# Full attention: values weighed for eight query blocks at once, in two part sums

## The reference

```python
qkv = h @ w_qkv.T                              # h: x after modulation
q, k, v = split(qkv, 3)                        # each (B, 16, T, 64)
s = q @ k.T * 64 ** -0.5 + rel_bias            # (B, 16, T, T); bias by clipped distance
p = softmax(s, axis=-1)
att = p @ v                                    # (B, 16, T, 64)
x = x + gate * (att.reshape(B, T, 1024) @ w_out.T)
```

## Time and profile before

| | |
|---|---|
| median of 3 runs | 2606.95 us (2600.77 to 2609.22) |
| the profiled execution | 2595.65 us, span 2593.9 us |
| busy over the span | PE 2449.6, PEld 1966.9, DVE 2153.8, ACT 2034.3, POOL 1519.8 us |
| stage of full attention | from 1655 to 2385.7 us of the span |
| mean granted TensorE clock | 0.986 |

### The profile page before, as it was taken

The page is one execution under the profiler, slowest core; times in us unless marked ns, Lnnn a source line. Parts: engine busy times, 40 slices in busy tenths (PEclk is TensorE's granted clock), DMA queues, the critical chain, the costliest instruction groups (busy, mean ns, idle before and its releaser), DMA issues. The chain is left out here.

```text
span 2593.9 us, 118567 instructions
## 1 busy us (share of the span) xinstructions
PE 2449.6 (94%) x52349; PEld 1966.9 (76%) x52349; DVE 2153.8 (83%) x2455; ACT 2034.3 (78%) x4077; POOL 1519.8 (59%) x1029
## 2 busy tenths in 40 slices
PE   6799999999999999999999999699999999997999
PEld 2478888888888888888888887467776776775787
DVE  5888888888888888888888886489898888885898
ACT  4788898889889899988888996667676666664776
POOL 3788887888888888888888884122222222222110
PEclk9999999999999999999999999899999999999999
DMA  3244433443444344334443332123232322221221
GB/s 96 51 99 94 109 78 93 94 108 84 98 94 111 82 94 99 95 84 94 101 97 83 91 85 60 43 48 68 46 70 50 67 47 66 51 57 31 83 74 41
DMA packets 275793, 202.01 MB, mean 78 GB/s; under 512 B 117568, under 2 KB 215880, under 8 KB 274248
## 3 DMA queue, kind: packets, MB, share of 16 engines
q1 hardware_dynamic: 275280, 194.42, 31.3%
HBM read 36.96 MB, written 1.11 MB: 15 GB/s over the span
## 5 line engine op out<-in xcount | busy, mean ns | idle before, releaser
L514 POOL TENSOR_TENSOR lt_t_sin<-lt_qk,lt_tab 128x512 f32<-128x512 f32 x384 | 685.1, 1805 | 225.1 <-DVE lt_qk L1296 222.8
L519 POOL TENSOR_TENSOR lt_qr<-lt_qr,lt_t_sin 128x1024 f32<-128x1024 f32 x192 | 457.7, 2384 | 28.1 <-POOL lt_t_sin L514 0.9
L2078 DVE TENSOR_REDUCE fa_neg_max<-bank 128x1 f32<-128x1024 f32 x256 | 301.6, 1220 | 90.7 <-PE bank L1875 89.1
L2000 ACT ACTIVATE fa_prob<-bank,fa_neg_max 128x1024 f32<-128x1024 f32 x128 | 142.6, 1114 | 215.7 <-DVE fa_neg_max L2078 163.4
L1901 PE MATMUL bank<-fa_prob_t,fa_v 32*64 32x128 f32 x16384 | 293.4, 276 | 16.8 <-issue 12.2
L1901 PEld LDWEIGHTS bank<-fa_prob_t,fa_v 32*64 32x64 f32 x16384 | 244.4, 130 | 78.1 <-issue 57.9
L2088 DVE STREAM_TRANSPOSE fa_prob_t<-fa_prob 128x1024 f32<-128x1024 f32 x256 | 302.1, 1218 | 0.0
L607 PE MATMUL bank<-lt_w_high,lt_x_high 128*128 128x512 f32 x576 | 262.2, 455 | 0.8 <-ACT lt_v_tok L1009 0.4
L977 ACT COPY lt_qk<-bank 128x512 f32<-128x512 f32 x384 | 224.5, 589 | 23.8 <-POOL lt_t_sin L514 2.8
L1296 DVE TENSOR_TENSOR lt_qk<-lt_qk,lt_rn 128x2048 f32<-128x2048 f32 x96 | 238.2, 2481 | 2.5 <-ACT lt_rn L1003 2.5
L1289 DVE TENSOR_REDUCE lt_ssq<-lt_qr 128x32 f32<-128x2048 f32 x96 | 218.9, 2281 | 24.7 <-ACT lt_qr L985 24.7
(11 more groups left out here) (260 smaller groups left out, 5857.0 us busy)
## 6 DMA issues: line engine op xcount, KB each, us to landing
lt_v<-lt_v_tok SPq DMA_DIRECT2D x576, 128.0 KB
fa_v<-fa_v_tok SPq DMA_DIRECT2D x256, 128.0 KB
lt_v<-lt_v_tok SPq DMA_DIRECT2D x192, 64.0 KB
lt_k_t<-lt_k_t SPq DMA_DIRECT2D x84, 128.0 KB, 2.9
lt_v<-lt_v SPq DMA_DIRECT2D x168, 64.0 KB, 2.1
lt_w_raw<-in_lt_wqkv_dram SPq DMA_DIRECT2D x36, 256.0 KB
ex_cw_all<-cw_kept SPq DMA_DIRECT2D x8, 1024.0 KB, 4.6
lt_x_s<-h_in SPq DMA_DIRECT2D x96, 64.0 KB, 2.8
```

The lines of the kernel that those rows point to most:

```text
L514: pool.tensor_tensor(dst[:, :, i, :], src[:, :, 1 - i, :], tab[:, g // 2 % 2, 1, at:at + 32].unsqueeze(1).to_broadcast([P, HEADS, 32]), AL ...
L519: pool.tensor_tensor(qr[:, g % 2, half], qr[:, g % 2, half], t_sin[:, :], ALU.add).then_inc(S.rotated, 1)
L2078: dve.tensor_reduce(neg_max[:, u % 2, par:par + 1], bank[:, 2 * par:2 * par + 2, :].rearrange("p a n -> p (a n)"), AX.X, ALU.max, negate=T ...
```

## The change

Values are weighed for a whole half (8 blocks) at once, a half late. A matmul has 256 moving columns in place of 128; a step has 32 of them in place of 64. The keys are summed in two parts of 512, each copied out by ScalarE (`empty_att`, at u % 4 of 3) into `h_mid`, a buffer that is free in this stage, and added by GpSimd before it divides. `prob_t` has one buffer in place of two, of the same size in all: step t of a half frees one eighth of it, and the next half's block t is written there, in a layout that alternates between even and odd halves. So `turn(u)` now waits at every step for the `weigh_v` of the same step. Projections come one at u % 4 of 0 (ahead of `weigh_v`), two at 2 and three at 3 (behind it); output products two at 1. Nothing cuts `weigh_v` any more. The reciprocals are turned once to a half and spread by transfers through memory (`widen_inverse`: 4 and 2 of them to a half), so `widen`, `spread_inverse` and `empty_inverse` are gone. There are 146 steps in place of 136.

```diff
-        prob_t = buf("prob_t", [P, 2, 2, UPQ, N])
...
+        prob_t = buf("prob_t", [P, 2, QB, QB, P])
...
         def jobs_at(u):
-            q, s = u // UPQ, u % UPQ
-            half = q // QPH + 1
-            if s == 1 or half >= HALVES:
+            half, first = u // QB + 1, (0, 1, 1, 3)[u % UPP]
+            if half >= HALVES:
                 return []
-            first = JPH * half + 6 * (q % QPH) + max(0, 2 * (s - 1))
-            return [first, first + 1]
+            first += JPH * half + 6 * (u % QB // UPP)
+            return [first + n for n in range((1, 0, 2, 3)[u % UPP])]
 
         def outs_at(u):
-            q = u // UPQ - 2
-            return [2 * q, 2 * q + 1] if u % UPQ == 1 and 0 <= q < QUADS else []
+            half = u // QB - (3 if u % QB == 1 else 2)
+            first = OUTS * half + (2 if u % QB == 1 else 0)
+            return [first, first + 1] if u % UPP == 1 and 0 <= half < HALVES else []
 
         def weighed_at(u):
 
-            q = u // UPQ - 1
-            return q if 0 <= q < QUADS else None
+            half = u // QB - 1
+            return half if 0 <= half < HALVES else None
...
-        STEPS = range(UNITS + 2 * UPQ)
...
+        STEPS = range(UNITS + 2 * QB + 2)
...
+                def widen_inverse(half):
+                    sp.wait_ge(S.inv_t, half + 1)
+                    if half >= 1:
+                        sp.wait_ge(S.inv_in, 32 * half)
+                    for a in range(4):
+                        sp.dma_start(inv_kept[:, 32 * a:32 * a + 32], inv_t[32 * a:32 * a + 2 * QB, :]).then_inc(S.inv_kept, 16)
+                    sp.wait_ge(S.inv_kept, 64 * (half + 1))
+                    if half >= 1:
+                        sp.wait_ge(S.att_t, half)
+                    for par in range(2):
+                        kept = inv_kept[QB * par:QB * par + QB, :].rearrange("(o u) q -> o (u q)", o=1)
+                        sp.dma_start(inv_all[HD * par:HD * par + HD, :], kept.to_broadcast([HD, N])).then_inc(S.inv_in, 16)
...
+                def divide(half):
+                    pool.wait_ge(S.att, 2 * half + 2)
+                    pool.tensor_tensor(att(1), att(0), att(1), ALU.add).then_inc(S.att_sum, 1)
+                    pool.wait_ge(S.att_sum, half + 1)
+                    pool.wait_ge(S.inv_in, 32 * (half + 1))
+                    if half >= 2:
+                        pool.wait_ge(S.out, OUTS * (half - 1))
+                    pool.tensor_tensor(att_t[:, half % 2, :].rearrange("p (u a r) -> p a u r", u=QB, a=4),
+                                       att(1).rearrange("p a (u r) -> p a u r", u=QB),
+                                       inv_all[:, :].rearrange("p (u a r) -> p a u r", u=QB, a=4),
                                        ALU.mult).then_inc(S.att_t, 1)
...
-                def weigh_v(q, s, n):
-
-                    half = q // QPH
-                    lo, step = KB // UPQ * s, KB // UPQ // 2
-                    if s == 0 and n == 0:
-                        pe.wait_ge(S.turned, 2 * UPQ * (q + 1))
-                        if q % QPH == 0:
-                            pe.wait_ge(S.v, 256 * (half + 1))
-                    for kb in range(lo + step * n, lo + step * (n + 1)):
+                def weigh_v(half, t):
+
+                    if t == 0:
+                        pe.wait_ge(S.turned, 2 * QB * (half + 1))
+                        pe.wait_ge(S.v, 256 * (half + 1))
+                    for i in range(KBS):
+                        kb, cols = KBS * t + i, slice(32 * i, 32 * i + 32)
                         for a in range(4):
                             rows = slice(32 * a, 32 * a + 32)
                             for par in range(2):
                                 d = slice(HD * par, HD * par + HD)
-                                mm = pe.matmul(bank[d, 4 + a, 0:P].rearrange("p (u r) -> p u r", u=UPQ),
-                                               v[rows, half % 2, kb, d],
-                                               prob_t[rows, q % 2, par, :, 32 * kb:32 * kb + 32],
-                                               start=kb == 0, stop=kb == KB - 1, skip_group_check=True)
-                    if n == 1:
-                        mm.then_inc(S.av, 1)
-
-                def spread_inverse(q):
-                    pe.wait_ge(S.wide_t, q + 1)
-                    if q == 0:
-                        pe.wait_ge(S.mean, 1)
-                    for a in range(4):
-                        rows = slice(32 * a, 32 * a + 32)
-                        for par in range(2):
-                            d = slice(HD * par, HD * par + HD)
-                            mm = pe.matmul(bank[d, 4 + a, P:2 * P].rearrange("p (u r) -> p u r", u=UPQ), mean_32[rows, :],
-                                           inv_t[rows, par, :, :], start=False, stop=True, skip_group_check=True)
-                    mm.then_inc(S.inv_all, 1)
+                                p = prob_t[rows, par, t, :, cols] if half % 2 else prob_t[rows, par, :, t, cols]
+                                mm = pe.matmul(bank[d, 4 + a, 0:JW].rearrange("p (u r) -> p u r", u=QB),
+                                               v[rows, half % 2, kb, d], p, start=kb % (KB // 2) == 0,
+                                               stop=kb % (KB // 2) == KB // 2 - 1, skip_group_check=True)
+                    mm.then_inc(S.av, 1)
...
-                    s, q = u % UPQ, weighed_at(u)
-
-
-                    fresh = s in (0, 3) or q is None
+                    s, half = u % UPP, weighed_at(u)
+
+
+                    fresh = s in (0, 3) or half is None
                     if u + 1 < UNITS:
                         scores(u + 1)
                     wait_emptied(pe, u - 1)
                     if s == 0:
                         for j in jobs_at(u):
                             job(j, fresh)
-
-                    outs, jobs = outs_at(u), jobs_at(u) if s >= 2 else []
-                    if q is not None:
-                        weigh_v(q, s, 0)
-                        if s in (1, 2):
-                            for n in outs[:1]:
-                                project_out(n, fresh)
-                            for j in jobs[:1]:
-                                job(j, fresh)
-                            outs, jobs = outs[1:], jobs[1:]
-                        weigh_v(q, s, 1)
-                        if s == 2:
-                            spread_inverse(q)
-                    for n in outs:
+                    if half is not None:
+                        weigh_v(half, u % QB)
+                    for n in outs_at(u):
                         project_out(n, fresh)
-                    for j in jobs:
-                        job(j, fresh)
+                    if s > 0:
+                        for j in jobs_at(u):
+                            job(j, fresh)
...
+                def empty_att(half, part):
+                    if half >= 1 and part == 0:
+                        act.wait_ge(S.att_t, half)
+                    act.copy(att(part), bank[:, 4:8, 0:JW]).then_inc(S.att, 1)
...
                 def turn(u):
-                    q = u // UPQ
-                    if u % UPQ == 0 and q >= 2:
-                        dve.wait_ge(S.av, UPQ * (q - 1))
+                    half, j = u // QB, u % QB
+                    if half >= 1:
+                        dve.wait_ge(S.av, QB * (half - 1) + j + 1)
                     for par in range(2):
                         dve.wait_ge(S.probs, 3 * u + 1 + 2 * par)
-                        dve.transpose(prob_t[:, q % 2, par, u % UPQ, :], prob[:, u % 2, par, :]).then_inc(S.turned, 1)
-
-                def invert(q):
-
-                    r = row_sum[:, q % 2, :, :]
-                    dve.wait_ge(S.probs, 3 * UPQ * (q + 1))
+                        if half % 2:
+                            dve.transpose(prob_t[:, par, :, j, :], prob[:, u % 2, par, :].rearrange("p (g n) -> p g n", g=QB))\
+                               .then_inc(S.turned, 1)
+                        else:
+                            dve.transpose(prob_t[:, par, j, :, :].rearrange("p g n -> p (g n)"), prob[:, u % 2, par, :])\
+                               .then_inc(S.turned, 1)
...
+                def turn_inverse(half):
+                    dve.wait_ge(S.inv, half + 1)
+                    if half == 0:
+                        dve.wait_ge(S.cleared, 1)
+                    else:
+                        dve.wait_ge(S.inv_kept, 64 * half)
+                    dve.transpose(inv_t[:, :], inv_sum[:, :]).then_inc(S.inv_t, 1)
...
+                    if u % QB == 0 and weighed_at(u) is not None:
+                        invert(weighed_at(u))
+                        turn_inverse(weighed_at(u))
```

146 lines of the change are left out of this document (56 added, 90 removed).

## The result

The kernel after the change takes **2626.5 us** (median of 5 runs, 2625.07 to 2629.82), the kernel before on the same chip 2600.77 (5 runs, 2599.34 to 2609.22). The ratio of the two is 1.0091, with a 95% interval of 1.0075 to 1.0108: the change made the kernel slower. The time lies in the range given; the ratio forecast was 1.0025.

A forecast was written before the change was run, and what follows sets the result against it. Bound: the chain of scores, maximum and exponential, a floor of 4.94 us a period (5.82 with bias). Steady +5, weighing +1, stalls -12, end +12.5 sum to +6.5 us: median about 2613.5, range 2599 to 2629.

The forecast's parts named there:

- the case with the largest chance: Whole kernel: slower than before by more than 0.3%, chance 0.43, against 0.41 within 0.3% and 0.16 faster.
- Weighing itself: `weigh_v` on TensorE: a wider piece costed at 2.02 us, 0 to 0.1 more, charged 1 us for the stage.
- The wait of a half's first step: VectorE waits 1.0 us for `weigh_v` before it may transpose, making that period 6.14 us.
- The fifth step's wait: The same wait at a half's fifth step costs nothing: bias moves the floor and there are no reciprocals.
- GpSimd's 5 us at the end of a half delay one low part: GpSimd's addition and product at a half's end: the delayed low part is wanted a step later, costed at nothing.
- The bias work: ScalarE rounds the bias behind three casts once to two halves, delaying an exponential about 0.5 us, 0.25 a half.
- Periods: Regular steps: floor of 4.94 us, 5.82 with bias, about 5.10 behind three projections; steady part +5 us.
- Stalls: Idle `weigh_v` matmuls released by nothing: half as many instructions leave more time per block, 12 of 13.3 us gone.
- The rival that they stay: Stalls in `weigh_v` are no matter of fetching or fall into longer matmuls too: +18.5 us, 2625, chance 0.22.
- The clock inside the loop: Sign of being wrong: a granted clock under full speed inside the loop.
- The end: Behind the last unit: eight pieces instead of four, 33 us against 20.3, +12.5 us.
- The start: Four more units without `weigh_v`, at the floor either way, clock already granted at 0.89: 0, give or take 1 us.

The follow-up runs named there:

- filling: Four matmuls of 256 columns, sums unread, added to each step without weighing: kernel after, 2623.38 us, ratio 1.0086; kernel before, 2594.06 us, ratio 0.9981.
- start and end mended: Kernel after with division, projection and small work moved, start filled, last output products in the scores' banks, last two divisions earlier: 2581.24 us, ratio 0.9914.

## Why the prediction was right, and where it was not

The median lies in the range, and the case with the largest chance, slower at 0.43, came. The mechanism of the regular periods and of the stalls was right, but that the time came out in the range was largely luck. The sum was +6.5 us, and it is +30.7 between the two profiled runs (+25.7 between the medians). The range reached so far up for stalls that stay; they went, and terms put at nothing or too low took their place. By its own steps:

- **Weighing itself**, 0 to 0.1 us a step more: it is 1.98 in place of 2.02, so the 1 us charged was not there. Halving the instructions alone doesn't shorten a piece.
- **The wait of a half's first step**: right in each number (copy 1.05, projection at 5.66, wait 1.0). The fifth step's wait costs nothing, as said.
- **"GpSimd's 5 us at the end of a half delay one low part"**, costed at nothing: this step failed, and it is the largest. Who waits for GpSimd was asked, and not whom its operations hold up. VectorE's addition does not end before GpSimd's product, 0.65 us in each of 14 halves, 9.1 in all; moving the product takes 9.3 back.
- **The bias work** was charged with 0.25 us a half, or 3.7; even halves take 1.27 more than odd ones, 8.9 in seven. ScalarE's rounding was counted about right: 0.60 in each of seven. VectorE's part was left out, 0.74 in each. About 0.5 of that is again GpSimd: a low part now falls beside the work and makes it 1.07 us in place of 0.58. The rest is lost cover: before the change the work fitted into a period of 5.35 that TensorE set, and now the period is 5.01.
- **Periods**: forecast 5.10 behind three projections, 4.94 elsewhere, 5.82 with bias. Measured 5.01, 4.88 to 5.01, and 5.80 to 5.88; over a half the difference is under 0.1 us. The mechanism of the earlier trace rows held.
- **Stalls**, -12 of 13.3: right in kind, for in weighing none is left in the middle. The rival that they stay falls: with twice the matmuls they return, 12 for 10.7 us. The Trainium skill (Runtime: NRT & Kernel Launch, Instruction fetch mechanics) says that crossing into a new block of instructions is mostly hidden. By count the traces agree, with 12 stalls in about 140 blocks before the change; but these 12 cost 10.7 us, so it doesn't follow from that sentence, as the rival had it, that the stalls are something else.
- **The clock inside the loop** was taken as full, and under full speed was named as a sign of being wrong. It came, in small: three stretches at half clock behind a long period, 3.3 us. With them the 13.3 us fell by 9.0, not by 12.
- **The end**, +12.5: it is +13.5, the 33 us are 34.0. Two sizes inside were off and offset each other: GpSimd's operations 2.00 in place of 2.4 and 2.5, and a pair of pieces behind the idle 3.39 us 5.05 in place of 3.8, at a lower clock.
- **The start**, 0 give or take 1: +5.1. Here the step failed that took the granted 0.89 as a fact of these steps. It was a result of how little TensorE had to do: four more steps without weighing brought it to 0.76 and 0.69, and filling to 1.00.

In sum: regular periods +21.1 in place of +6, stalls and half clock in the middle -9.0 in place of -12, end +13.5 in place of +12.5, start +5.1 in place of 0: 30.7, and what lies ahead of and behind the stage cancels.

## What to carry to other kernels

When a change shortens the engine that hid some small work, list that work by step: it appears on the path wherever its cover was set by that engine, and it can often be moved to a step that still has a margin, which here, with the division and one projection moved too, turned +0.9% into -0.25% and, with start and end mended, into -0.9%. Of that, filling alone gives the kernel before 0.2%. When a large operation is moved on GpSimd, look at what VectorE does at that moment, not only at who waits for the result. And where a pipeline gets longer by a stage, price its start and end with the clock that their idle engine will be granted.
